# Sequence attention: row sums from pairs of key tiles added on VectorE and GpSimd, finished one or two groups later

## The reference, cut to what matters

```python
def _L1_xattn_ref(q, k, v, gamma):        # q = layernorm(x), k = v = ctx, (8, 256, 512) each
    h = 8; dq = dv = 256 // h             # 8 heads of 32, taken from the 256 rows
    qh, kh = q.reshape(B, h, dq, 512), k.reshape(B, h, dq, 512)
    vh = v.reshape(B, h, dv, 512)
    qk = jnp.einsum('bhdq,bhdl->bhql', qh, kh) / sqrt(dq)
    sm = jax.nn.softmax(qk, axis=-1)                      # over 512 keys l
    ret = jnp.einsum('bhql,bhdl->bhdq', sm, vh).reshape(B, 256, 512)
    return gamma * ret
x = x + _L1_xattn_ref(_layernorm(x), ctx, ctx, gamma)
```

## Time and profile before

| | |
|---|---|
| profiled execution | 1560.04 us, span 1558.2 us |
| sequence attention, first `maximum` to last store | about 723 to 1037 us of the span |
| busy of the span | TensorE 1388.9 us (89%), VectorE 806.3 (52%), ScalarE 728.5 (47%), GpSimd 481.5 (31%) |
| `outputs` and `sums` | 512 matmul records each, in 64 sets of eight each |

### The profile page before, as it was taken

How to read it: one execution, slowest core, us unless ns; L and a number is a source line. 1 busy time by engine, 2 the same in 40 slices (tenths; PEclk the granted TensorE clock), 3 DMA queues, 4 the chain that set the end, 5 groups by cost and what they waited for, 6 DMA issues and landing times. The chain is left out here.

```text
span 1558.2 us, 22502 instructions
## 1 busy us (share of the span) xinstructions
PE 1388.9 (89%) x8434; PEld 662.8 (43%) x8434; DVE 806.3 (52%) x1312; ACT 728.5 (47%) x1364; POOL 481.5 (31%) x522
## 2 busy tenths in 40 slices
PE   4788888788868999996899999989999999999998
PEld 4455555554533444552222222234444444444443
DVE  5864666566655878765666666624513211321220
ACT  3266666667664777771555555553501211210210
POOL 7211111446675775771322232144600000000000
PEclk9699999999988999997899999999999999999999
DMA  6646655656332010122644443223502002001000
GB/s 179 136 138 174 142 146 172 152 111 155 113 122 81 28 41 28 42 84 66 170 137 123 123 125 114 97 82 111 173 0 82 1 1 81 0 0 54 0 1 27
DMA packets 89446, 140.68 MB, mean 90 GB/s; under 512 B 8408, under 2 KB 47896, under 8 KB 88800
## 3 DMA queue, kind: packets, MB, share of 16 engines
q1 hardware_dynamic: 76544, 114.16, 26.8%
q10 hardware_dynamic: 12800, 25.17, 5.2%
HBM read 105.85 MB, written 33.46 MB: 89 GB/s over the span
## 5 line engine op out<-in xcount | busy, mean ns | idle before, releaser
L1785 DVE TENSOR_REDUCE c_negmax<-c_psA 128x1 f32<-128x512 f32 x256 | 165.7, 682 | 91.5 <-PE c_psA L1860 87.1
L2071 ACT ACTIVATE d_silu<-d_psGU 128x512 f32<-128x512 f32 x64 | 38.2, 596 | 344.3 <-PE d_psGU L2138 344.3
L2138 PE MATMUL d_psGU<-d_zt_hi,d_w_hi 128*128 128x512 bf16 x512 | 194.6, 380 | 3.8 <-ACT d_silu L2071 2.3
L2138 PE MATMUL d_psGU<-d_zt_hi,d_w_lo 128*128 128x512 bf16 x512 | 194.8, 380 | 0.0
L2138 PE MATMUL d_psGU<-d_zt_lo,d_w_hi 128*128 128x512 bf16 x512 | 194.8, 380 | 0.0
L1740 ACT ACTIVATE c_probs<-c_psB 128x512 f32<-128x512 f32 x256 | 140.4, 595 | 101.5 <-PE c_psB L1873 101.4
L2101 DVE TENSOR_TENSOR d_h<-d_psGU,d_silu 128x512 f32<-128x512 f32 x64 | 44.2, 691 | 221.2 <-PE d_psGU L2138 220.9
L894 DVE TENSOR_REDUCE a_negmax<-a_psX 128x4 f32<-128x1024 f32 x128 | 150.7, 1215 | 7.8 <-PE a_psX L1161 7.8
L753 ACT ACTIVATE a_probs<-a_psB 128x512 f32<-128x512 f32 x256 | 138.2, 593 | 24.8 <-PE a_psB L1173 24.5
L1860 PE MATMUL c_psA<-c_ks,c_qs 96*128 96x512 bf16 x256 | 103.8, 408 | 16.5 <-DVE c_negmax L1785 8.1
L672 POOL TENSOR_SCALAR ternary<-a_tern_stage 128x512 bf16<-128x512 f32 x48 | 91.6, 1924 | 77.4 <-ACT a_tern_stage L741 77.1
(11 more groups left out here) (231 smaller groups left out, 2559.0 us busy)
## 6 DMA issues: line engine op xcount, KB each, us to landing
a_tern_stage<-in_w ACTq DMA_DIRECT2D x32, 768.0 KB, 5.5
d_weight_stage<-in_w_last SPq DMA_DIRECT2D x24, 512.0 KB, 4.2
a_ks<-k_scr SPq DMA_DIRECT2D x8, 768.0 KB
a_qs<-q_scr SPq DMA_DIRECT2D x8, 768.0 KB
c_ks<-k_scr SPq DMA_DIRECT2D x48, 128.0 KB, 2.6
c_qs<-q_scr SPq DMA_DIRECT2D x48, 128.0 KB, 3.0
a_xz<-in_x SPq DMA_DIRECT2D x32, 128.0 KB, 3.1
a_ctx<-in_ctx_t SPq DMA_DIRECT2D x8, 512.0 KB, 4.7
```

The source lines that it names most:

```text
L1785: v.tensor_reduce(negm[:, u:u + 1], A[:, u % 2, :], AX.X, ALU.max, negate=True)\
L2138: last = pe.matmul(GU[:, 2 * up + i % 2, :], wgu[wh][:, i, up, k, :], zt[zh][:, k, :], start=(k == 0 and j == 0), stop=(k == DC - 1 and j ...
```

## The change

The exponentials go to `c_probs` with four steps in place of two. In each quad VectorE adds steps 0 and 1 (after r5), and GpSimd adds steps 2 and 3 (once all exponentials of step 3 are there), each into one half of a new tile `c_prob_pairs`, as one TENSOR_TENSOR of 128x2048 f32. TensorE sums the pairs: the first half in step 2, the second in step 0 of the next quad. The last quad of all sums its steps 2 and 3 one by one. Steps 1 and 3 have no `sums`. The rest of a quad's end moves: `results` after the exponentials of step 1 of the next quad, behind the second `sums`; `turn_sums` in step 2, reciprocals still after r9; `turn_recips` in step 0 of the quad after that; `finish` there after r1; `update` later by a quad too. GpSimd's order in a batch becomes `update`(q-2), `normalised`, `spread`(q-1), `context_low`, add of q, `low`, `update`(q-1), `spread`(q), add of q+1.

```diff
-        pr = sb("c_probs", [P, 2, 4, D], F32)
+        pr = sb("c_probs", [P, 4, 4, D], F32)
+        pairs = sb("c_prob_pairs", [P, 2, 4, D], F32)
...
+        def added(engine, unit, quads, pair, done):
+            engine.wait_ge(s["exp_done"], MQ * quads + 8 * (pair + 1))
+            need(engine, s["sums_done"], 2 * quads + pair - 1)
+            unit.tensor_tensor(pairs[:, pair].rearrange("p j q -> p (j q)"), pr[:, 2 * pair].rearrange("p j q -> p (j q)"),
+                               pr[:, 2 * pair + 1].rearrange("p j q -> p (j q)"), ALU.add).then_inc(done, 1)
...
             def attend(b, par, n, m):          # GpSimd
+                k = 2 * b
+                if k >= 2:
+                    update(k - 2)
                 if m is not None:
                     front.normalised(pool, m)
-                if not begins(b):
-                    spread(b - 1, 1)
+                if k:
+                    spread(k - 1)
                 if m is not None:
                     front.context_low(pool, m)
-                    front.low(pool, m)
-                if not begins(b):
-                    update(b - 1, 1)
                 if n is None:
                     following.scales(pool, 0)
-                spread(b, 0)
-                update(b, 0)
+                added(pool, g, k, 1, s["pair_pool"])
+                if m is not None:
+                    front.low(pool, m)
+                if k:
+                    update(k - 1)
+                spread(k)
+                if k + 1 < LAST:
+                    added(pool, g, k + 1, 1, s["pair_pool"])
...
                     if j == 0:                 # ScalarE, exponentials
-                        need(act, s["pv_done"], EG * b + e - 1)
-                    act.activation(pr[:, e % 2, j, :], B[:, j % 2, :], ACT.Exp, scale=HD1 ** -0.5)\
+                        need(act, s["pv_done"], EG * b + e - 3)
+                        if e % 2 == 0:
+                            need(act, s["pair_pool" if e % 4 else "pair_dve"], (EG * b + e) // 4)
+                    act.activation(pr[:, e % 4, j, :], B[:, j % 2, :], ACT.Exp, scale=HD1 ** -0.5)\
...
             def results(b, quad):
                 act.wait_ge(s["pv_done"], EG * b + QT * (quad + 1))
+                act.wait_ge(s["sums_done"], 2 * (2 * b + quad + 1))
...
-                    if e == QT:
+                    if e == 1 and not begins(b):
+                        results(b - 1, 1)
+                    if e == QT + 1:
                         results(b, 0)
...
                     for k in range(QT):        # VectorE
                         if n is not None:
                             maxima(n, quad, range(4 * k, 4 * k + 2))
-                        if ends and k == 1:
-                            reciprocals(*last)
-                        if ends and k == 3:
-                            finish(*last)
+                        if q >= 2 and k == 0:
+                            finish(q - 2)
+                        if q and k == 2:
+                            reciprocals(q - 1)
+                        if k == 1:
+                            added(dve, v, q, 0, s["pair_dve"])
...
+            def sums(k, pair):                 # TensorE; pv_done now comes from outputs
+                if pair:
+                    pe.wait_ge(s["pair_pool"], k + 1)
+                else:
+                    need(pe, s["ret_done"], k - 1)
+                    pe.wait_ge(s["pair_dve"], k + 1)
+                for j in range(4):
+                    last = pe.matmul(OS[32 * j:32 * j + 32, k % 2, 1, :], keep["ones"][:, 0:32], pairs[:, pair, j, :],
+                                     start=(pair == 0), stop=(pair == 1))
+                last.then_inc(s["sums_done"], 1)
...
-                    if i == 1 and (quad or not begins(b)):
-                        turn_sums(*last)
-                    if i == 3 and (quad or not begins(b)):
-                        turn_recips(*last)
+                    if i == 0 and q >= 2:
+                        turn_recips(q - 2)
+                    if i == 2 and q:
+                        turn_sums(q - 1)
...
                         elif turn == 5:
-                            sums(b, e)
+                            if i == 0 and q:
+                                sums(q - 1, 1)
+                            if i == 2:
+                                sums(q, 0)
+                            if q == LAST and i >= 2:
+                                last_sums(e)
```

More of the change, by code:

```diff
@@ L1690, in first, with spread @@
                 front.low(pool, 1)
-            def spread(b, quad):
-                k = 2 * b + quad
+            def spread(k):
                 pool.wait_ge(s["recip_done"], k + 1)
@@ L1773, in attend @@
                     exponentials(n, 0)
-                results(b, 1)
             run(act, first, attend)
+            results(BATCH - 1, 1)
         @block.vector
@@ L1801, in reciprocals, with finish @@
                     .then_inc(s["recip_done"], 1)
-            def finish(b, quad):
-                k = 2 * b + quad
+            def finish(k):
+                quad = k % 2
                 dve.wait_ge(s["recip_turned"], k + 1)
@@ L1818, in attend @@
                 for quad in range(2):
-                    last = (b, 0) if quad else (b - 1, 1)
-                    ends = quad == 1 or not begins(b)
+                    q = 2 * b + quad
                     if begins(b) and quad == 0:
@@ L1845, in _ @@
             run(dve, first, attend)
-            reciprocals(BATCH - 1, 1)
-            finish(BATCH - 1, 1)
+            finish(LAST - 1)
+            reciprocals(LAST)
+            finish(LAST)
         @block.tensor
@@ L1882, in outputs @@
                     o = (4 * (e // QT) + j) * HD1
-                    pe.matmul(OS[32 * j:32 * j + 32, e // QT, 0, :], vt[par][:, kt, o:o + HD1], pr[:, e % 2, j, :],
-                              start=(kt == 0), stop=(kt == QT - 1))
-            def sums(b, e):
-                kt = e % QT
-                if kt == 0:
-                    need(pe, s["ret_done"], 2 * b + e // QT - 1)
-                for j in range(4):
-                    last = pe.matmul(OS[32 * j:32 * j + 32, e // QT, 1, :], keep["ones"][:, 0:32], pr[:, e % 2, j, :],
+                    last = pe.matmul(OS[32 * j:32 * j + 32, e // QT, 0, :], vt[par][:, kt, o:o + HD1], pr[:, e % 4, j, :],
@@ L1898, in turn_sums, with last_sums @@
+            def last_sums(e):
+                for j in range(4):
+                    last = pe.matmul(OS[32 * j:32 * j + 32, 1, 1, :], keep["ones"][:, 0:32], pr[:, e % 4, j, :],
+                                     start=False, stop=(e == EG - 1))
+                if e == EG - 1:
+                    last.then_inc(s["sums_done"], 1)
+            def turn_sums(k):
+                pe.wait_ge(s["os_copied"], k + 1)
                 for a in range(QT):
-                    last = pe.transpose(OS[:, quad, 1, a * P:(a + 1) * P], os_sb[:, quad, 1, a * P:(a + 1) * P], keep["ident"][:])
+                    last = pe.transpose(OS[:, k % 2, 1, a * P:(a + 1) * P], os_sb[:, k % 2, 1, a * P:(a + 1) * P], keep["ident"][:])
@@ L1900, in turn_sums, with turn_recips @@
                 last.then_inc(s["sums_turned"], 1)
-            def turn_recips(b, quad):
-                pe.wait_ge(s["recip_spread"], 2 * b + quad + 1)
+            def turn_recips(k):
+                pe.wait_ge(s["recip_spread"], k + 1)
                 for a in range(QT):
-                    last = pe.transpose(OS[:, quad, 1, a * P:(a + 1) * P], rb[:, a * P:(a + 1) * P], keep["ident"][:])
+                    last = pe.transpose(OS[:, k % 2, 1, a * P:(a + 1) * P], rb[:, a * P:(a + 1) * P], keep["ident"][:])
@@ L1957, in _ @@
             run(pe, first, attend)
-            turn_sums(BATCH - 1, 1)
-            turn_recips(BATCH - 1, 1)
+            turn_recips(LAST - 1)
+            turn_sums(LAST)
+            turn_recips(LAST)
 def build_gated_ffn(nc, io, keep, x_in, out, front):
```

21 lines of the change are left out of this document (12 added, 9 removed).

## The result

| kernel | median of its runs, us | ratio to the kernel before, 95% interval |
|---|---|---|
| before (the three runs above and one more) | 1564.83 (1561.67 to 1566.96) | |
| changed | 1602.3 (1599.2 to 1602.88) | 1.0237 [1.0222, 1.0251] |

The change made the kernel slower by 37 us. The forecast was 1579, with a range of 1556 to 1592: the sign was right, the size was not, and the time lies above the range. The profiled execution of the changed kernel took 1599.2 us, span 1597.1.

The account below looks back on a forecast made before the run. TensorE sets the pace, not by far. Five batches at 0.3 (late reduces) + 2.8 (blocked split) + 0.7 (clock) give +19.0; other batches make it +16.9 on 1560.0: 1577, put at 1579 us, range 1556 to 1592.

Parts of the forecast that it names:

- The sets: TensorE's `sums`: 64 sets become 33, at 1.09 us each, 33.8 us saved if nothing else became late.
- VectorE's add: The add of steps 0 and 1 on VectorE in each quad, taken at 2.29 us (2.29 to 2.6).
- M8 late: TensorE's matmul block 8 for the maxima waits for VectorE's reduce 6, behind the add: 2.0 us even quad, 1.8 odd.
- M4 of the even quad: TensorE's matmul block 4 for the maxima waits for VectorE's reduce 2, behind `finish` and statistics: 1.9 us instead of 0.73.
- The moved work of SyncE: SyncE's transfers of halves and shifts run later, into the odd quad; priced at nothing, 1 to 2 us a batch if queued.
- the walk: Step-by-step timing of an odd and an even quad: removed work eaten by VectorE's lateness, +0.3 us a batch.
- The block at the split: At the even quad's end, GpSimd's add and `low` block VectorE's split of the maxima; TensorE waits 2.8 us at `shifts`.
- the point left open: Whether GpSimd's add also blocks the split's CAST on VectorE: assumed from the skill's rule, shown by no row.
- TensorE's clock: The 2.8 us stall at `shifts` may bring TensorE to 1.2 GHz: 0.7 us a batch (0 to 1.7).
- Rival 4: Clock falls in every quad behind the 2 us waits for reduces: 11 more stretches at 1 us, 1590 us; chance 0.1.
- GpSimd's add: The add of steps 2 and 3 on GpSimd in each quad: 3.85 us, no more than 5.1.
- Rival 1: VectorE's reduces keep up and TensorE's saving survives: 1540 us with half of the waits, 1530 with all saved; chance 0.12.

Follow-up runs that it names:

- experiment 2: Against the changed kernel, VectorE adds nothing: steps 0 and 1 are summed one by one, GpSimd still adds steps 2 and 3; 1596.1 us.
- Experiment 3: The changed kernel with matmuls whose result nobody reads put into TensorE's waits; 1587.2 us.
- experiment 1: Against the changed kernel, GpSimd adds nothing: steps 2 and 3 are summed one by one, VectorE still adds steps 0 and 1; 1599.0 us.
- experiment 7: The changed kernel with GpSimd's add of each even quad made to wait until VectorE has taken the split of the maximums; 1602.2 us.
- experiment 4: The changed kernel with GpSimd's add of 2048 columns made as four operations of 512; 1589.1 us.
- experiment 5: The changed kernel with both TensorE's waits filled with unused matmuls and GpSimd's add in four pieces of 512; 1579.3 us.
- Version 9: Against the changed kernel, GpSimd adds steps 0 and 1, VectorE steps 2 and 3 behind the split; sums, statistics, `high` and shift transfers also moved; 1542.5 us.
- Experiment 11: The kernel with the adds swapped, but its statistics together again after r1 instead of behind r4, r8 and r10; 1545.1 us.
- experiment 10: The kernel with the adds swapped, plus GpSimd's `low` ahead of `update` in the odd quad; 1541.3 us.
- experiment 12: Adds swapped and `low` ahead of `update`, plus SyncE writing the halves out ahead of the two 512 KB loads; 1537.8 us.

## Why the prediction was right in sign and too small

**Held, step by step.** The sets: 31 fewer, and each that is left is listed with 1.06 us at full clock (1.09 forecast). VectorE's add: 2.28 us where it meets nothing, 2.35 in the mean (2.29). M8 late by 2.03 and 1.80 (2.0 and 1.8), M4 of the even quad by 1.83 (1.9), of the odd one by 0.23 (0.4). The moved work of SyncE, priced at nothing: in the steady batches no wait for it. Quads without any half clock show the walk best: even ones take 19.28 us, and 18.51 - 2.18 - 0.38 + 1.2 + 2.0 is 19.15. The block at the split, too: the CAST and the TENSOR_TENSOR were held up one after the other, the second by `low`, which got in between. By the Trainium skill, SBUF — State Buffer, section Who interferes with whom, a cast can be blocked in this way as well; the trace agrees (1.21 us in place of 0.17, 2.87 in experiment 2), which was the point left open.

**Failed: TensorE's clock.** The step said "I take 0.7 (0 to 1.7)" a batch. Each of the five steady batches holds two stretches of 3.4 us at 1.2 GHz; an even quad with one takes 20.88 us, one without 19.28, so one behind M8 costs 1.6. One behind the turn costs about 1.2 (an estimate: 23.75, less 20.96 for the same quad with the idle filled, less 1.6). Experiment 3 puts the batch at 2.4: less than two stretches, because behind a slow even quad the turn waits 2.25 us in place of 3.32. Two things were wrong. I counted only the 2.8 us wait as one that may bring the clock down, but eight of the ten stretches stand behind the 2 us waits at M8. And so I took 1.7, the price of one stretch, as the end of the range for a batch that has two. That part of a stretch lies inside a wait fits the one behind the turn (1.2), but behind M8 TensorE is what is waited for, and all of it counts. Rival 4 had the mechanism, at chance 0.10 and with 1 us a stretch; its 1590 is too low as well. Of the 13.4 us by which the steady batches are above the forecast, 5 x (2.4 - 0.7) = 8.5 are this term. One such stretch is also most of batch 6's error, 1.4 longer instead of 0.7 shorter.

**Mis-sized: GpSimd's add.** 3.85 forecast, 4.53 measured, inside the bound of 5.1. Behind an even quad at full clock the turn starts 4.38 us after O, where the forecast had 0.88 + 2.8 = 3.68: 0.7 later, as much as the add is longer, and 3.5 us in five batches. Where the even quad was itself longer by a stretch at half clock, the split came later within the add and the turn waited 2.25 us; that gain is already counted in the 2.4. Most of the last 1.4 us is M8: from start to start it comes 2.20 and 1.97 us late, 0.2 more than forecast in each quad (the rows give the idle time, which is shorter, since matmuls overlap at their ends). The straight line through shorter shapes was the weak part of the estimate of the add. The Trainium skill, GPSIMD Engine Reference, section Elementwise — side-by-side cycle accounting, gives 4.5 us for an add of this length on GpSimd and 2.3 on VectorE, and the trace agrees with both (4.53 and 2.28).

**Wrongly joined: the terms as a sum.** The forecast adds up waits as if each could be taken away for its price. The runs show that some overlap: either add alone costs 34 to 36 us (experiments 1 and 2), and taking the block away at the split gives nothing, as the second `sums` then waits 2.66 us (experiment 7). Others nearly add up: the clock and the block are worth 15 and 13 us apart and 23 together (experiments 3, 4 and 5). This bears on what an edit can win back; the forecast's total fails by the terms above.

**Rival 1** did not come true here, but its times, 1540 and 1530 with the reduces kept up, are about what another order allows: the same two adds a quad, put where VectorE and GpSimd are free, reach 1538.

**Left open.** Version 9 moved several things at once. Experiment 11 shows that the statistics' place is worth 3 to 4 us of its 60; how the rest falls on the adds' exchange, the place of the two `sums` and that of `high` was not taken apart. A pair of adds in bf16 wasn't tried. And why the clock stays at full in some quads with the same two waits (the one from 836.00) is not known. Nor does the length of the wait alone settle it: in version 9 waits of 1.23 to 1.72 us for the transfer left the clock at full in four even quads, and in the fifth, with one of 1.58, it fell.

## What to carry to other kernels

Before work is moved to an engine with spare time, look up what the bottleneck waits for, and put the new operation behind that, in the stretch where the engine would idle: here the same two adds cost 37 us in one place and, with the orders around them adapted, gained 22 to 28 in another. Price each wait of TensorE with the clock that follows it: where it fell behind a wait of 2 us, that made 1.6 us more. And keep long GpSimd operations, and any queued behind them, away from the moment at which VectorE has a short operation on the critical path.

## What the runs showed of the hardware

- GpSimd's f32 add of 128x2048 takes 4.53 us; from 1.27 (512) and 2.13 (1024) a straight line gives 3.85. Four of 512 take 4.94.
- A CAST of 128x16, 0.17 us by itself, took up to 2.87 while GpSimd's add ran (0.80 with the add in four pieces), and the TENSOR_TENSOR behind it 2.04 behind a GpSimd operation that was already queued.
- In quads with TensorE busy 15 to 17 of 19 to 21 us, waits of 1.8 to 2.0 us at M8 were in eight of ten followed by 3.4 us at 1.2 GHz, and filling them with matmuls kept the clock at 1.00 (experiment 3).
- A 256 KB write issued behind two 512 KB loads let the step that waits for it begin 5.9 us after the issue; issued ahead of them, 2.8 us (one odd quad of each, experiments 10 and 12).
